# Context and targets' features in two f16 parts for the output projection, and a first stage in another order

## What is computed

```python
h = jnp.maximum(_layernorm(x, axis=-1), 0.0)
hs = layer_norm(h, ln1_scale, ln1_bias); ht = layer_norm(h_target, ln1_scale, ln1_bias)
q = (ht @ Wq + bq).reshape(T, H, HD) / sqrt(HD)
k = (hs @ Wk + bk).reshape(S, H, HD); v = (hs @ Wv + bv).reshape(S, H, HD)
logits = jnp.where(edge_mask[None] != 0, jnp.einsum('thd,shd->hts', q, k), NEG)
ctx = jnp.einsum('hts,shd->thd', softmax(logits), v).reshape(T, D)
ht = ht + (ctx @ Wo + bo)
ht = layer_norm(ht, ln2_scale, ln2_bias)
y = x + ht + gelu(ht @ W1) @ W2
```

## Time and profile before

| | us |
|---|---|
| median of 3 runs | 690.22 (690.02 to 692.46) |
| the profiled execution | 694.41 |
| its span | 692.6 |
| PE busy | 657.6 (95%) |
| DVE busy | 569.2 (82%) |
| POOL busy | 524.2 (76%) |
| ACT busy | 484.0 (70%) |

### The profile page before, as it was taken

How to read it: one execution, slowest core, us unless ns; L and a number is a source line. 1 busy time by engine, 2 the same in 40 slices (tenths; PEclk the granted TensorE clock), 3 DMA queues, 4 the chain that set the end, 5 groups by cost and what they waited for, 6 DMA issues and landing times. The chain is left out here.

```text
span 692.6 us, 20346 instructions
## 1 busy us (share of the span) xinstructions
PE 657.6 (95%) x8346; PEld 473.0 (68%) x8346; DVE 569.2 (82%) x946; ACT 484.0 (70%) x932; POOL 524.2 (76%) x488
## 2 busy tenths in 40 slices
PE   4898999999999999999999999999999899899998
PEld 4465667766776777677767766777777567557767
DVE  5987899989999879999997798989868888575661
ACT  4865668766778858677787686778866788867550
POOL 3574889889999957899998678999977777471430
PEclk9998999999999999999999999999999999999999
DMA  8735501113001011220011112012000000000001
GB/s 296 258 80 153 177 31 36 59 63 108 2 2 34 2 62 63 58 82 2 2 33 33 62 33 78 17 51 74 2 2 2 2 3 2 1 1 32 24 17 54
DMA packets 20797, 36.23 MB, mean 52 GB/s; under 512 B 2752, under 2 KB 13280, under 8 KB 20704
## 3 DMA queue, kind: packets, MB, share of 16 engines
q1 hardware_dynamic: 20704, 34.92, 16.2%
HBM read 26.49 MB, written 2.10 MB: 41 GB/s over the span
## 5 line engine op out<-in xcount | busy, mean ns | idle before, releaser
L1412 POOL TENSOR_TENSOR prob_lo<-prob 128x512 f16<-128x512 f32 x382 | 437.1, 1169 | 74.1 <-ACT prob L888 73.2
L888 ACT ACTIVATE prob<-score 128x512 f32<-128x512 f32 x512 | 304.1, 597 | 135.8 <-PE score L469 128.3
L469 PE MATMUL score<-nidentb,mask_nat 128*128 128x128 bf16 x2048 | 199.1, 220 | 4.1 <-ACT qT L905 1.9
L469 PE MATMUL early<-kT,qT 96*128 96x512 f16 x512 | 192.9, 382 | 10.5 <-DVE half_max L1203 10.1
L469 PEld LDWEIGHTS ctx<-v_sb,prob 128*128 128x128 bf16 x2048 | 159.0, 98 | 60.2 <-ACT raw L910 12.6
L469 PE MATMUL score<-qT,kT 97*128 97x512 f16 x512 | 196.3, 383 | 0.0
L1203 DVE CUSTOM_DVE_ANT_0 early<-early,mask_nat,half_max 128x1024 f32<-128x1024 f32 x128 | 163.6, 1287 | 38.0 <-PE early L469 36.0
L469 PE MATMUL ctx<-v_sb,prob 128*128 128x65 f16 x2048 | 191.4, 193 | 2.3 <-ACT raw L910 1.8
L469 PE MATMUL ctx<-v_sb,prob_lo 128*128 128x65 f16 x2048 | 190.4, 193 | 0.0
L469 PEld LDWEIGHTS ctx<-v_sb,prob_lo 128*128 128x128 f16 x2048 | 142.6, 97 | 49.9 <-issue 4.0
L1203 DVE CUSTOM_DVE_ANT_0 early<-early,mask_nat 128x1024 f32<-128x1024 f32 x128 | 157.1, 1229 | 22.5 <-PE early L469 20.8
(11 more groups left out here) (167 smaller groups left out, 623.2 us busy)
## 6 DMA issues: line engine op xcount, KB each, us to landing
adj_in<-in_adj SPq DMA_DIRECT2D x26, 512.0 KB, 4.0
qT<-q_stage SPq DMA_DIRECT2D x48, 64.0 KB, 2.0
kT<-mask_nat SPq DMA_DIRECT2D x48, 64.0 KB, 2.0
raw<-in_x SPq DMA_DIRECT2D x4, 512.0 KB, 5.6
tgt<-in_L_gnn_h_target SPq DMA_DIRECT2D x4, 512.0 KB, 11.6
prob<-in_adj SPq DMA_DIRECT2D x4, 512.0 KB, 10.4
nT<-in_L_gnn_W SPq DMA_DIRECT2D x2, 1024.0 KB, 6.6
mask_nat<-in_x SPq DMA_DIRECT2D x1, 2048.0 KB, 8.3
```

What stands on the lines that cost most here:

```text
L469: return nc.tensor.matmul(dst, w, m, start=start, stop=stop, **more)
L888: nc.scalar.activation(prob[:, n % SLOTS, :], score[n % 2][:, :], ACT.Exp).then_inc(exp_done, 1)
L1412: nc.gpsimd.tensor_tensor(prob_lo[:, n % SLOTS, :], prob[:, n % SLOTS, :], prob_hi(n % SLOTS), ALU.subtract).then_inc(lo_sem["pool"], 1)
```

## The change

The first stage: on PE `project(2)` comes ahead of `turn_rows(3)`, 24 unread products stand in front of it, the early pairs 0 and 1 come ahead of `project(4)`, and `shift_row(0)` ahead of the tenth early pair. POOL masks chunk 1 before it norms chunk 2. ACT's `features(2)` comes ahead of `deviation(2)`. Both `target_deviation` calls move from there into step 3 of unit 1. On DVE `target_stats(1)` moves behind the tenth maximum, `target_stats(2)` into unit 0 and the two `target_norm` into unit 1.

The output projection: the context, the targets' features and `wo` are each held as a high and a low part in f16. ACT writes the high parts, DVE the low parts of context and features, POOL that of `wo`. A row tile is then six f16 products of 256 columns (high x high, high x low, low x high, for two chunks) and four of 128 with the f16 identity. The features in f32 lie in `t_full`, the parts in the buffers that held them.

```diff
@@ -47,7 +47,7 @@
...
-WIDE, UNREAD = 64, 20
+WIDE, UNREAD, UNREAD_LATER = 64, 20, 24
@@ -65,6 +65,12 @@
...
+T_HIGH = {0: [(1, 1), (1, 2)], 1: [(3, 8), (3, 14)]}
+T_LOW = {0: [(1, 2), (1, 3)], 1: [(5, 1), (5, 5)]}
+WO_UNIT = 2
@@ -192,6 +198,7 @@
...
         wo = sb("wo", [P, DC, D], F32)
+        wo_parts = sb("wo_parts", [P, 2, DC, D], F16)
         ident32 = sb("ident32", [P, P], F32)
@@ -205,9 +212,6 @@
...
         node_b = sb("node_b", [P, NT], BF16)
...
         cols = sb("cols", [P, 10, DC], F32)
@@ -228,6 +232,9 @@
...
         src = raw[:, :, :].rearrange("p k c -> p (k c)")[:, 0:NT * D].rearrange("p (t d) -> p t d", d=D)
@@ -235,6 +242,12 @@
...
+        t_full = [nTq[:, 1, :, :], cT[:, :, :], cT[:, :, :], cT[:, :, :]]
...
+        t_parts = [nTq[:, i, :, :].rearrange("p c t -> p (c t)").bitcast(F16).rearrange("p (r c t) -> p r c t", r=2, c=DC)
+                   for i in range(2)]
+        c_parts = cT[:, :, :].rearrange("p c t -> p (c t)").bitcast(F16).rearrange("p (r c t) -> p r c t", r=2, c=DC)
         wkv = cT[:, :, :].rearrange("p c t -> p (c t)").rearrange("p (k c d) -> p k c d", k=2, c=DC)
@@ -252,7 +265,7 @@
...
                       for i in range(2))
-        h_bufs = [nTq[:, 0, :, :].rearrange("p c t -> p (c t)").bitcast(F16).rearrange("p (r c t) -> p r c t", r=2, c=DC),
+        h_bufs = [t_parts[0],
                   qT[:, 0, 0:4, :].rearrange("p h t -> p (h t)").rearrange("p (r c t) -> p r c t", r=2, c=DC)]
@@ -294,6 +307,7 @@
...
         q_hi = sem("q_hi")
+        t_hi, t_lo, c_hi, wo_hi, wo_lo = sem("t_hi"), sem("t_lo"), sem("c_hi"), sem("wo_hi"), sem("wo_lo")
         w_in, w_hi, w_lo = [sem(f"w_in{i}") for i in range(2)], sem("w_hi"), sem("w_lo")
@@ -502,7 +516,7 @@
...
                             w = wq[:, c, m * P:(m + 1) * P] if what == "t0" else wkv[:, 0, c, m * P:(m + 1) * P]
-                            r = nTq[:, 0, c, :] if what == "t0" else nT[:, what, c, :]
+                            r = t_full[0][:, c, :] if what == "t0" else nT[:, what, c, :]
                             last = mm(proj_bank(g, m), w, r, c == 0, c == DC - 1)
@@ -628,12 +642,18 @@
...
                         aux_free(("wo", k, t // 2))
+                    if t == 0:
+                        pe.wait_ge(wo_lo, 1)
+                        pe.wait_ge(t_lo, DC * (k + 1))
                     dst = aux[:, t % 2 * D:(t % 2 + 1) * D]
+                    part = slice(t * P, (t + 1) * P)
                     for c in range(DC):
-                        mm(dst, cT[:, c, t * P:(t + 1) * P], wo[:, c, :], c == 0, False, skip_group_check=True)
+                        for a, w in ((0, 0), (0, 1), (1, 0)):
+                            mm(dst, c_parts[:, a, c, part], wo_parts[:, w, c, :], c == a == w == 0, False, skip_group_check=True)
                     for c in range(DC):
-                        last = mm(dst[:, c * P:(c + 1) * P], nTq[:, k % 2, c, t * P:(t + 1) * P], ident32[:, :], False,
-                                  c == DC - 1, skip_group_check=True)
+                        for a in range(2):
+                            last = mm(dst[:, c * P:(c + 1) * P], t_parts[k % 2][:, a, c, part], ident16[:, :], False,
+                                      c == DC - 1 and a == 1, skip_group_check=True)
                     if t % 2 == 1:
@@ -647,7 +667,7 @@
...
                         aux_free(("qp", k, m))
-                    last = mm(aux[:, :], wq[:, c, m * P:(m + 1) * P], nTq[:, k % 2, c, :], c == 0, c == DC - 1)
+                    last = mm(aux[:, :], wq[:, c, m * P:(m + 1) * P], t_full[k][:, c, :], c == 0, c == DC - 1)
                     if c == DC - 1:
@@ -688,21 +708,24 @@
...
                 values(0)
+                for i in range(UNREAD_LATER):
+                    mm(early[1][:, TB:TB + P], identb[:, :], identb[:, :], True, True)
+                project(2)
                 turn_rows(3)
-                project(2)
                 values(1)
...
                 project(3)
-                values(2)
-                for i in range(2):
-                    early_scores(0, i)
-                project(4)
-                for e in range(1, RAMP + 2):
+                for e in range(2):
                     for i in range(2):
                         early_scores(e, i)
-                    if e + 2 < NT // 2:
-                        values(e + 2)
-                shift_row(0)
+                project(4)
+                for e in range(2, RAMP + 2):
+                    if e == RAMP + 1:
+                        shift_row(0)
+                    for i in range(2):
+                        early_scores(e, i)
+                    if e < NT // 2:
+                        values(e)
                 for n in range(AHEAD):
@@ -843,7 +866,7 @@
...
                         if what == "t0":
-                            dst, bias = nTq[:, 0, c, :], RES_B
+                            dst, bias = t_full[0][:, c, :], RES_B
                             act.wait_ge(res_b, 1)
@@ -930,7 +953,10 @@
...
                     job_here("cT", k, c)
-                    nc.scalar.activation(cT[:, c, :], aux[:, :], ACT.Copy).then_inc(aux_done, 1)
+                    if c == 0 and k + 1 < NTB:
...
+                        act.wait_ge(t_lo, DC * (k + 2))
+                    nc.scalar.activation(c_parts[:, 0, c, :], aux[:, :], ACT.Copy).then_inc(c_hi, 1)
@@ -958,7 +984,24 @@
...
                     job_here("qT", k, c)
-                    affine(nTq[:, k % 2, c, :], aux[:, :], LN1_G[:, c:c + 1], RES_B[:, c:c + 1]).then_inc(aux_done, 1)
+                    affine(t_full[k][:, c, :], aux[:, :], LN1_G[:, c:c + 1], RES_B[:, c:c + 1]).then_inc(aux_done, 1)
...
+                def feature_high(k, c):
+                    if k == 0:
+                        act.wait_ge(nT_done, c + 1)
+                    else:
+                        act.wait_ge(aux_done, AUX["qT", k, c] + 1)
+                    if c == 0:
+                        if k == 1:
...
+                            act.wait_ge(t_lo, DC)
+                        if k > 1:
...
+                            act.wait_ge(aux_ready, AUX["wo", k - 2, 1] + 1)
+                    nc.scalar.activation(t_parts[k % 2][:, 0, c, :], t_full[k][:, c, :], ACT.Copy).then_inc(t_hi, 1)
...
+                def output_high():
+                    nc.scalar.activation(wo_parts[:, 0, :, :], wo[:, :, :], ACT.Copy).then_inc(wo_hi, 1)
@@ -997,22 +1040,20 @@
...
                 rectify(3)
+                features(2)
                 deviation(2)
                 high_parts(1)
-                features(2)
+                high_values(0)
                 deviation(3)
                 last_sources()
-                high_values(0)
+                high_parts(2)
                 features(3)
-                high_parts(2)
                 high_values(1)
...
                 high_parts(3)
-                for k in range(1, 3):
-                    target_deviation(k)
                 nc.scalar.activation(warm_c, eps_c, ACT.Exp).then_inc(act_link, 1)
+                high_parts(4)
                 high_values(2)
-                high_parts(4)
                 feature_sum(0)
@@ -1038,6 +1079,15 @@
...
                             row_out(u + 1)
+                        if u == 1 and s == 3:
+                            for b in (1, 2):
+                                target_deviation(b)
+                        if k == 0 and (r, s) in T_HIGH[0]:
+                            feature_high(0, T_HIGH[0].index((r, s)))
+                        if k + 1 < NTB and (r, s) in T_HIGH[1]:
+                            feature_high(k + 1, T_HIGH[1].index((r, s)))
+                        if u == WO_UNIT and s == 6:
+                            output_high()
                         if s == 6 and u in HIGH_AT:
@@ -1183,6 +1233,15 @@
...
+                def feature_low(k, c):
+                    dve.wait_ge(t_hi, DC * k + c + 1)
+                    parts = t_parts[k % 2]
+                    nc.vector.tensor_tensor(parts[:, 1, c, :], t_full[k][:, c, :], parts[:, 0, c, :], ALU.subtract).then_inc(t_lo, 1)
...
+                def context_low(k, c):
+                    dve.wait_ge(c_hi, DC * k + c + 1)
+                    nc.vector.tensor_tensor(c_parts[:, 1, c, :], aux[:, :], c_parts[:, 0, c, :], ALU.subtract).then_inc(aux_done, 1)
@@ -1281,31 +1340,30 @@
...
                 second_stats(2)
+                low_parts(0)
                 second_scale(2)
...
                 second_scale(3)
-                low_parts(0)
                 low_parts(1)
                 low_values(0)
+                make_mask(0, 0)
+                low_parts(2)
+                for i in range(1, TT):
+                    make_mask(0, i)
+                low_values(1)
+                low_parts(3)
+                maxima(0)
+                maxima(1)
+                low_parts(4)
+                maxima(2)
+                low_values(2)
+                make_mask(0, 4)
+                maxima(3)
+                make_mask(0, 5)
```

(40 more changed lines are left out.)

6 lines of the change are left out of this document (3 added, 3 removed).

## The result

The changed kernel takes 702.52 us (median of 6 runs, 701.12 to 703.74), the kernel before 691.34 beside it on the same chip (6 runs, 689.96 to 694.53): ratio 1.0149, 95% interval 1.0116 to 1.0182. It is slower by 11 us, where 689.3 was forecast and 694.5 was the upper end.

A forecast was written before the change was run, and what follows sets the result against it. PE sets the pace, DVE close behind. Terms -5.0 - 5.2 + 4.1 + 3.9 + 1.3 + 0 gave -0.9 us, 693.5 against the profiled 694.41; carried to the median, 689.3. Own range 686.8 to 693.7, outer 684.5 to 694.5.

The forecast's parts named there:

- Carrying over: Last step of the sum: the median lies 4.2 us below the profiled run, and this difference was carried to the forecast.
- Rival 2: Slower, 694: half-clock stretches at PE's waits before `project(3)` and the first scores take back head gain; chance 0.18.
- Head, -5.0: First stage: new order and full clock start the first context product near 67.0 instead of 72.01; gain 5.0 us.
- Output rows, -0.43 each: Output projection on PE: an f16 row takes 0.88 us instead of 1.31; 16 rows, 5.2 in units, 1.7 in feed-forward.
- Features' low parts, +3.9: DVE subtractions in r = 5, blocks 0 to 2: 1.3 us lost per block, 3.9 in all; bounds 2.1 and 5.7.
- a lag of 0.8 is allowed: In r = 5, DVE may come 0.8 us late before PE's next early pair waits.
- Context's low parts, +4.1: r = 2: PE waits for DVE's low part through `aux`, and maxima lag; 4.1 us in all, bounds 2.8 and 5.2.
- Unit 1, +1.3: Table switches for the moved roots stop exp 2.9 us in unit 1; loss 1.3 us, bounds 0.8 and 2.6.
- DVE catches up: Unit 1: during PE's stand of about 2.7 us for the roots, DVE gets its new work done.
- Output weights, `target_stats(2)`, at nothing: Splitting output weights on POOL and ACT, and statistics moved to unit 0, cost nothing; the statistics 0.9 without room.
- Tail, 0: After the units: up product 1.7 us later for the context's low part, four rows give 1.7 back; bounds -1.0, +1.5.
- Rival 1: Faster, 685: DVE's new work hides in its idle time, stalls take their lower ends, sum -5.5; chance 0.31.

The follow-up runs named there:

- roots_late: before_warm with the two target-deviation square roots and their reciprocals moved into unit 1; 694.36 us, ratio 1.0033 to the kernel before.
- head_only: The kernel before with only the new first stage, output projection still in f32; 694.54 us, ratio 1.0026 to the kernel before.
- low_on_pool: The changed kernel with the features' low parts subtracted on POOL instead of DVE, at other steps; 696.30 us, ratio 1.0060 to the kernel before.
- both_a: before_warm's first stage plus f16 parts, features' low parts on POOL, first turned context earlier, output weights' parts in unit 0; 689.82 us, ratio 0.9971 to before.
- both_b: both_a with the second turned context a step earlier and one low part of prob moved from DVE to POOL in r = 2 and 4; 688.85 us.
- before_warm: The kernel before plus 84 unread products on PE in the first stage, where its profiled run fell to half clock; 690.75 us, ratio 0.9981.

## Why the prediction was wrong

Summed against its own time, the profiled 694.41, it had -0.9 us; the profiled run of after stands at +6.7. That is 7.6 us of mis-sized terms. The rest of the distance from 689.3 to 702.5 is 4.2 us of carrying the difference over to the median and 1.4 us, since the median of after is a run of clock 0.998.

- **Carrying over.** The step that failed first, and it is one of arithmetic. The head's 5.0 us were counted from a run with two stretches at half clock, and their larger part was the clock's return. Then the difference between the profiled run and the median, 4.2 us, was carried over whole to the forecast. But the median, 690.22, is the time of a run at full clock, below the profiled one just because it lacks those stretches. A gain was taken from time that the median didn't contain. Rival 2 names this ("The timed runs may also have lacked half-clock stretches"), and the sum left it out.
- **Head, -5.0.** Measured -3.28 to the first context product (68.73 for 67.0), and some 1.2 late against a run of before at full clock (by the estimate of 67.5). The order saves nothing of its own. `project(2)` starts at 29.34, as forecast (29.1), and PE waits 1.52 us ahead of `project(3)`, as allowed for; but it also waits 0.58 ahead of `turn_rows(4)` and 0.55 for the placement of the keys by a DMA, and neither was in the working. The step that failed for the scores is "`high_values(7)` ends only near 59.7". In the new order `values(7)` comes behind its early pair, on PE from 58.69; ACT can read it only at 60.61, and `negated(0)` follows at 61.78, 2.1 us late. So scores begin at 63.14 where 61.1 was forecast. The maxima couldn't end "near 58" either, with the last pair itself at 58.3: the eighth ended at 60.4, which still was early enough.
- **Output rows, -0.43 each.** Right: 248.13 to 249.0 is 0.87 for the forecast 0.88, and r = 3, with two of them, is 0.84 shorter.
- **Features' low parts, +3.9.** Measured 7.3. The place was right, and so was +1.2 in r = 5. The step that failed is "a lag of 0.8 is allowed": it is allowed once, and then the lag is still there in r = 6, whose 1.17 us of idle time come too late for it. The size per operation was 1.25 and not 0.98, the rest being time in which POOL's instruction was still running.
- **Context's low parts, +4.1.** 1.59 and twice 0.59 more in r = 2, with the 0.87 of two rows back: 2.46 + 1.46 + 1.46 = 5.4. Block 1 was right (1.7 net forecast, by PE's wait at step 5). In blocks 2 and 3 the wait at step 5 was 0.41 (0.6 forecast), but the lag behind it cost 1.0 each and not 0.3 and 0.1.
- **Unit 1, +1.3.** Measured 1.23, with two table loads and PE's wait of 2.33 where 2.7 was forecast. "DVE catches up" failed: the same pause makes units 2 and 3 longer, 1.5 us in roots_late, 2.0 in after with the casts. Both units were outside the working, which took five units for all. The pair of loads costs 2.05 us in a run at full clock, not 1.3. From the last exp's end at 89.12 to the next at 92.23 are 3.1 us for both. The Trainium skill (ScalarE: Activation LUTs, What ACT_TABLE_LOAD costs) gives 2.66 us for one switch, of which some 1.28 are the load and the rest a drain. The trace agrees on the load, 1.28 us each, and not on the sum: two switches and both roots took 3.1 us.
- **Output weights, `target_stats(2)`, at nothing.** Right for `target_stats(2)`: roots_late without the move has the units 2 and 3 of head_only with it. The output weights were not separated by a run of their own. low_on_pool has 2.9 us in units 1 to 3, head_only 2.2 without parts. The 0.7 between them has to be ACT's casts, POOL's feature parts or the output weights in unit 2; both_a has 0.05 there, with casts and feature parts in unit 1, the output weights in unit 0 and the roots in the first stage. That speaks for the output weights and is argued, not shown.
- **Tail, 0.** Right: +2.41 of wait for the low part against the rows and what was hidden; the tails are equal to 0.1 us, and without the low part the tail is 1.7 shorter, the 1.7 that stood in the sum on either side.
- The rivals: the slower one (694) had the right sign, but not the mechanism: it put the loss on half-clock stretches of the changed kernel, and the change is 11 us slower with both kernels at full clock. Rival 1 fell at r = 5 and r = 2, as its own "against" had it.

The terms now: rows -5.2, features +7.3, context +5.4, unit 1 +1.2, units 2 and 3 +2.0, -0.6 in r = 1 (its cause is open): +10.1 in the units, which is 531.55 - 521.50.

## What to carry to other kernels

Count a gain only against the runs that are to be compared: if the profiled run is slower than the timed ones because of the granted clock, what the clock gives back is not in the timed runs. Work laid on the second engine of a chain costs its own length less the idle time that stands between it and the next thing that is waited for; idle time further on takes nothing. So follow the lag through the units behind, and give the work to the engine and unit that has its idle time just there: both_b keeps the f16 parts, with the old first stage and the unread products of before_warm, and is 0.5% faster than before (2.8 us with both at full clock), where the change as made is 1.5% slower.
